# Four blocks over 32 images: the 32x128 TensorE tiling replaced by 64-row and strip forms, rounding moved from ScalarE to GpSimd

## The chip, the core and the metric

One NeuronCore of a Trainium2 chip runs the whole program; the other seven are idle. The metric is the device time of one execution in microseconds (us). TensorE (PE) does the matmuls, VectorE (DVE), ScalarE (ACT) and GpSimd (POOL) the elementwise work, and SyncE (SP) issues the DMAs.

## The reference

The input `x` is 32 images of 128 channels by 1024 positions (fp32). Each image goes through four blocks:

```
L0: xn = group_norm(x, 8 groups);  q,k,v = xn Wq, xn Wk, xn Wv (+bias), width 128
    x  = softmax(q k^T / sqrt(128)) v Wp + bp + xn
L1: t  = group_norm(x, 32 groups); 8 heads of width 16
    x  = concat_h softmax(q_h k_h^T / 4) v_h  Wp + bp + x
L2: h  = instance_norm(x);         one head of width 128
    x  = x + softmax(q k^T / sqrt(128)) v
L3: Qn, Kn = l2-normalised 16-wide projections over channels; V = 128-wide projection
    x  = gamma * (sum_n V + Qn^T (Kn V^T)) / (N + Qn^T (sum_n Kn + eps))
```

## The kernel before

Everything of an image lives in SBUF as 128 partitions (channels) by 1024 columns (positions); the images are software-pipelined. Each image is cut into some 500 small steps, named in `STEPS`: `f_*` are the full-width attentions L0 and L2 (argument `layer` 0 or 2), `p_*`, `m_*`, `s_*`, `o_*` the eight-head attention L1, `t_*` the last block L3. The table `TIME` gives each step a moment relative to its image's start, and image i stands `PERIOD` later than image i-1. `play()` sorts all steps of all images by that moment, and each engine issues its own part of each step in that order. So the table sets only the order in which each in-order engine meets its work; semaphores do the rest.

PSUM is shared by name: `P_CHAIN` (one bank) holds all small products in turn, `P_MAX` the scores of which only the row maximum is wanted, `P_SC` and `P_FULL` scores and outputs of the full-width attentions, `P_HEAD` and `P_ACC` those of the heads. A TensorE step waits until the step before it on the same bank has been read (`chain_free`, `max_free`), so a late reader holds up TensorE and all that is queued on it.

Precision. Two kinds of matmul occur. Where the operands are fp32r (rounded fp32) a matmul is one pass over its columns. Where they are plain fp32, the trace has two records for one matmul and the columns are streamed four times. The full-width attentions use split operands: `hi` is the value rounded to fp32r and `lo` the remainder, and a product is hi·hi + hi·lo + lo·hi. For each half of q, k and v (steps `f_qk`/`f_value`, and `p_qk` for the heads) TensorE writes the projection into `P_CHAIN`; ScalarE reads it twice, once into `hi` (L827, L847, L863) and once into the single SBUF tile `exact` (L837, L854, L869); GpSimd then subtracts, `lo = exact - hi` (L719, L726, L752). `exact` is one tile for all: the next copy into it waits for the subtraction before.

TensorE tilings. A matmul whose operands fill only part of the 128x128 array is placed in a part of it. In this kernel four classes occur: 128x128 (full), 64x128 (`m_max`, `s_scores`: two head pairs side by side in the row halves), 128x32 (`s_pv`, `f_sums`, `m_turn`, `t_matrix`, `t_turn`: results of up to 32 partitions, four side by side in `s_pv`) and 32x128 (`o_spread`, `f_spread`, `t_ksum`, `t_out`: contractions over 16, 2 or 17 rows). In the profile's rows the pair before the shape (`17*128`, `128*17`) is rows times columns of the operand held in the array, from which the class follows.

L3 in short: `t_project` makes q, k, v per token, `t_matrix` sums k v^T over eight groups of 128 tokens into a 17x129 matrix, `t_keep` copies it to `ma`, `t_ksum`/`t_scale` make the divisor, `t_turn` transposes the scaled queries (eight 128x17 pieces), `t_out` multiplies `ma` by them.

Of the kernel before, what the change touches and what calls it, by code (L numbers as in the profile page):

```python
# [6 lines left out]
F32R = mybir.dt.float32r  # L7
# [4 lines left out]
C = 128  # L12
N = 1024
# [15 lines left out]
FULL_ROW = {0: 64, 2: 96}  # L29

PERIOD = 206.000
# [23 lines left out]
    t_ksum=(), t_scale=(), t_turn=(range(2),), t_turned=(range(2),), t_out=(range(2),),  # L55
# [3 lines left out]
    load=[-444.568],  # L59
    g_stat=[-342.954],  # L60
    g_average=[-329.385],
    g_var=[-327.831],
    g_apply=[-327.403],
    f_qk=[-324.62, 236.025, -318.173, 237.463, -316.071, 239.499, -307.845, 240.328],
# [12 lines left out]
    f_scores=[-263.28, 268.702, -261.043, 270.662, -258.57, 285.892, -252.49, 288.403, -250.371,
        290.772, -247.938, 299.63, -242.481, 304.009, -237.548, 308.313, -228.304, 316.719,
        -222.89, 321.314, -216.238, 323.033, -213.85, 329.623, -209.464, 331.03, -206.509, 334.796,
        -204.968, 343.181, -191.73, 346.525],  # L80
    f_less=[-266.355, 269.509, -263.662, 270.173, -262.719, 281.768, -260.687, 289.64, -256.216,
        291.082, -245.343, 298.521, -241.05, 301.934, -238.661, 302.674, -229.65, 308.912,
        -228.073, 317.519, -222.928, 321.041, -219.107, 323.554, -214.199, 325.222, -204.373,
        329.575, -195.645, 335.975, -187.214, 341.895],
    f_exp=[-268.223, 264.621, -258.987, 269.397, -257.31, 277.163, -251.224, 287.023, -247.696,
        292.071, -247.182, 295.201, -244.469, 301.093, -241.845, 302.139, -235.507, 308.569,
        -231.815, 311.103, -229.246, 316.026, -215.475, 316.504, -209.673, 321.277, -201.534,
        325.812, -188.334, 331.546, -185.442, 335.653],
    f_plo=[-253.636, 261.779, -247.912, 262.733, -243.882, 285.896, -243.223, 290.654, -242.148,
        293.919, -240.27, 300.114, -238.771, 307.496, -237.402, 308.425, -236.979, 309.735,  # L90
        -232.01, 318.166, -230.727, 318.184, -230.13, 334.62, -224.858, 343.112, -204.25, 347.219,
        -187.48, 350.979, -178.415, 355.211],
    f_add=[-233.808, 279.161, -251.331, 262.822, -244.056, 290.409, -242.413, 291.769, -242.043,
        295.383, -240.22, 303.539, -237.966, 307.617, -237.194, 309.239, -279.97, 258.722,
        -234.087, 310.608, -231.148, 318.787, -229.752, 335.525, -205.881, 344.174, -195.077,
        347.242, -194.2, 355.122, -191.606, 358.969],
    f_pv=[-258.564, 276.685, -252.295, 276.718, -249.065, 291.543, -246.2, 295.985, -241.646,
        304.458, -235.005, 308.326, -228.594, 317.236, -222.453, 320.625, -214.672, 323.529,
        -213.821, 330.323, -209.242, 331.088, -205.083, 337.021, -201.343, 345.473, -187.722,
        349.286, -176.874, 350.007, -172.212, 352.561],  # L100
# [25 lines left out]
    m_max_read=[-85.592, -82.44, -80.627, -73.34, -72.457, -68.925, -63.823, -62.141, -60.424,  # L126
# [1416 lines left out]
```

## Time and profile before

| | us |
|---|---|
| three runs | 6186.26, 6187.2, 6193.69 (median 6187.2) |
| the profiled execution, its own time | 6179.77 |
| its span, first to last instruction | 6178.0 |
| mean granted TensorE clock | 0.979 |
| HBM read / written | 18.13 MB / 16.78 MB |

The profile is one execution. "Busy" counts the time in which an engine has an instruction in flight; TensorE's ends are modelled, so two neighbouring matmuls overlap in the rows and the distance from one start to the next is what one costs.

### The profile page before, as it was taken

What the parts mean: (1) busy time and instruction counts of PE and PEld (TensorE: products, weight loads), DVE (VectorE), ACT (ScalarE), POOL (GpSimd) and SP (SyncE); (2) the same over time, 40 slices, a digit from 0 to 9 for tenths busy, and PEclk for the clock granted to TensorE, in tenths of its full rate; (3) what the DMA queues carried; (4) which work ended last, traced back from release to release, by engine and by line L of the source; (5) the groups of instructions that cost most, each with busy time, mean ns of one, the idle gap of its engine ahead of it and who ended that gap; (6) DMA issues with size and microseconds to landing.
All of it is one profiled execution on the core that took longest, in us unless ns stands there. A gap on an engine that the chain in (4) does not pass through costs nothing.

```text
span 6178.0 us, 82441 instructions
## 1 busy us (share of the span) xinstructions
PE 5741.7 (93%) x28818; PEld 2690.0 (44%) x28818; DVE 4620.2 (75%) x5748; ACT 4141.6 (67%) x5764; POOL 3426.0 (55%) x2739
## 2 busy tenths in 40 slices
PE   5789999999999999999999999999999999999885
PEld 2334444444444444444444444444444444444332
DVE  2677777777777777777777777777777777777752
ACT  2367777766777676777766767767677777677652
POOL 4336655556665555655555666555565555566433
PEclk7899999999999999999999999999999999999996
DMA  1011101011101101111101110110110110111000
GB/s 36 4 27 24 29 21 30 20 31 24 31 19 30 31 20 31 24 25 25 29 21 31 24 31 19 30 30 21 31 24 21 29 30 20 31 24 31 16 17 8
DMA packets 103485, 154.27 MB, mean 25 GB/s; under 512 B 63776, under 2 KB 66080, under 8 KB 102944
## 3 DMA queue, kind: packets, MB, share of 16 engines
q1 hardware_dynamic: 103072, 149.00, 11.1%
q8 instruction: 230, 3.77, 0.3%
q14 instruction: 183, 1.50, 0.1%
HBM read 18.13 MB, written 16.78 MB: 6 GB/s over the span
## 4 chain that ended last, share of the span: by engine, by line
PE 72%; DVE 16%; ACT 5%; issue 3%; POOL 3%; DMA 0%; SPq 0%; DVEq 0%; POOLq 0%; ACTq 0%
PE p_max L1251 16%; PE p_chain L1251 15%; PE p_sc L1251 12%; PE p_full L1251 11%; PE p_acc L1251 9%; PE p_head L1251 8%; DVE mx_half L1066 8%; ACT p L930 3%; DVE f2mx L1061 2%; DVE fp L1107 2%; POOL x L787 1%; POOL fsum L781 1%; POOL fp_lo L760 1%; DVE f_num L1125 1%; DVE t_dn L1198 1%
## 5 line engine op out<-in xcount | busy, mean ns | idle before, releaser
L1066 DVE TENSOR_REDUCE mx_half<-p_max 128x2 f32<-128x1024 f32 x2048 | 2506.8, 1224 | 891.1 <-PE p_max L1251 883.1
L930 ACT ACTIVATE p<-p_head 128x1024 f32<-128x1024 f32 x2048 | 2094.8, 1023 | 1103.0 <-PE p_head L1251 1047.8
L760 POOL TENSOR_TENSOR fp_lo<-fp,fp_hi 128x512 fp32r<-128x512 f32 x1024 | 1311.6, 1282 | 734.1 <-ACT fp L894 732.5
L781 POOL TENSOR_TENSOR fsum<-fsum,fp 128x512 f32<-128x512 f32 x768 | 987.9, 1286 | 282.3 <-ACT fp L894 282.1
L1251 PE MATMUL p_max<-ks,qs 63*128 63x512 f32 x4096 | 993.9, 481 | 102.0 <-DVE mx_half L1066 80.3
L1251 PE MATMUL p_acc<-p,v 128*17 128x512 f32 x8192 | 1080.9, 601 | 7.8 <-ACT p L930 7.6
L1251 PE MATMUL p_head<-qs,ks 64*128 64x512 f32 x4096 | 938.9, 454 | 43.6 <-ACT p L930 26.5
L892 ACT ACTIVATE fp_hi<-fp 128x512 fp32r<-128x512 f32 x1024 | 641.4, 626 | 367.3 <-DVE fp L1107 261.6
L1107 DVE TENSOR_TENSOR fp<-p_sc,f_shifts 128x512 f32<-128x512 f32 x1024 | 700.1, 684 | 147.5 <-PE p_sc L1251 60.3
L1251 PEld LDWEIGHTS p_max<-ks,qs 63*128 63x128 f32 x4096 | 385.8, 185 | 921.5 <-DVE mx_half L1066 736.3
L1251 PEld LDWEIGHTS p_head<-qs,ks 64*128 64x128 f32 x4096 | 385.7, 185 | 679.5 <-issue 385.8
L894 ACT ACTIVATE fp<-fp 128x512 f32<-128x512 f32 x1024 | 634.2, 619 | 0.0
L1061 DVE TENSOR_REDUCE f0mx<-p_max 128x1 f32<-128x1024 f32 x256 | 312.2, 1220 | 136.4 <-PE p_max L1251 136.2
L777 POOL TENSOR_TENSOR fsum<-fp 128x512 f32<-128x512 f32 x128 | 164.1, 1282 | 427.6 <-ACT fp L894 427.6
L1061 DVE TENSOR_REDUCE f2mx<-p_max 128x1 f32<-128x1024 f32 x256 | 312.5, 1221 | 104.2 <-PE p_max L1251 104.2
L1251 PEld LDWEIGHTS p_acc<-p,v 128*17 128x17 f32 x8192 | 144.6, 95 | 328.3 <-issue 282.2
L1251 PE MATMUL p_sc<-f2q_hi,f2k_hi 128*128 128x512 f32 x512 | 253.6, 495 | 35.0 <-DVE fp L1107 31.3
L1251 PE MATMUL p_sc<-f0q_hi,f0k_hi 128*128 128x512 f32 x512 | 251.0, 490 | 19.9 <-DVE fp L1107 17.9
L1251 PE MATMUL p_full<-fp_hi,f0v_hi 128*128 128x512 f32 x512 | 242.6, 474 | 2.7 <-POOL fp_lo L760 2.7
L1251 PE MATMUL p_full<-fp_hi,f2v_hi 128*128 128x512 f32 x512 | 228.7, 447 | 5.9 <-POOL fp_lo L760 5.9
L1251 PE MATMUL p_max<-f2k_hi,f2q_hi 128*128 128x512 f32 x512 | 187.7, 448 | 29.2 <-DVE f2mx L1061 17.4
L1251 PE MATMUL p_max<-f0k_hi,f0q_hi 128*128 128x512 f32 x512 | 185.2, 444 | 24.8 <-DVE f0mx L1061 17.2
(187 smaller groups left out, 7977.6 us busy)
## 6 DMA issues: line engine op xcount, KB each, us to landing
qs<-cq_hi SPq DMA_DIRECT2D x128, 256.0 KB, 4.8
ks<-ck_hi SPq DMA_DIRECT2D x128, 256.0 KB, 4.7
x_in<-x_dram SPq DMA_DIRECT2D x32, 512.0 KB, 4.4
qs<-cq_lo SPq DMA_DIRECT2D x64, 256.0 KB, 4.4
ks<-ck_lo SPq DMA_DIRECT2D x64, 256.0 KB, 5.1
out_dram<-x SPq DMA_DIRECT2D x32, 512.0 KB, 5.3
o<-o SPq DMA_DIRECT2D x256, 32.0 KB, 2.0
zrow<-rz SPq DMA_DIRECT2D x128, 16.0 KB
```

Source lines behind the costliest of these rows:

```text
L760: pool.tensor_tensor(fp_lo[u % 2][:, :], fp[u % 2][:, :], f32(fp_hi[u % 2][:, :]), ALU.subtract).then_inc(f.plo, 1)
L777: pool.tensor_tensor(dst, fp[(u - 1) % 2][:, :], fp[u % 2][:, :], ALU.add)\
L781: pool.tensor_tensor(dst, dst, fp[u % 2][:, :], ALU.add).then_inc(f.sum, 1)
L787: pool.tensor_tensor(x3[:, :], f_num[:, :], x2[:, :], ALU.add)\
L892: act.activation(fp_hi[u % 2][:, :], fp[u % 2][:, :], ACT.Exp, scale=float(C) ** -0.5).then_inc(f.p, 1)
L894: act.activation(fp[u % 2][:, :], fp[u % 2][:, :], ACT.Exp, scale=float(C) ** -0.5).then_inc(f.pexact, 1)
L930: act.activation(p1[slot][:, 2 * pr:2 * pr + 2, :], P_HEAD[:, :].rearrange("p (e n) -> p e n", e=2), ACT.Exp, scale=float(DH) ** -0.5).the ...
L1061: dve.reduce_max(f_mx[layer][:, v:v + 1], P_MAX[:, :], AX.X).then_inc(sem.max_read, 1)
L1066: dve.reduce_max(mx_half[:, pr, :, t, kh], P_MAX[:, :].rearrange("p (e n) -> p e n", e=2), AX.X)\
L1107: dve.tensor_tensor(fp[u % 2][:, :], P_SC[:, :], f_shifts[:, :], ALU.add)\
L1125: dve.tensor_tensor(f_num[:, q], f_num[:, q], P_CHAIN[:, :], ALU.mult)\
L1251: return pe.matmul(dst, lhsT, rhs, start=start, stop=stop)
```

## The change

It does four things.

1. No matmul uses 32x128 any more. `f_spread` and `o_spread` contract over 64 rows (zero rows are added: `zrow` and `spread_r` become 128 rows, the two layers share rows 64 and 65). `t_matrix` writes its matrix four times, once into each 32-column strip; `t_keep` copies all 128 rows; the new GpSimd step `t_spots` multiplies the matrix by four masks (`strips`) into `ma_spots`; `t_turn` becomes two full 128x128 transposes of queries padded to 32; `t_out` becomes four full matmuls of 128 columns for each half.
2. `mm32` writes an fp32 matmul as four 32-column strips where the matmul before it in the order was of the class 128x32, and as one full matmul otherwise.
3. ScalarE makes only the `exact` copy of a projection; GpSimd first rounds `exact` into `hi` (a new instruction, CAST) and then subtracts for `lo`. This holds for all sixteen projection halves of an image.
4. All numbers of `TIME` are new (of the table one or two lines are shown), `PERIOD` is 205.92 for 206.0, and two semaphores per layer become one counter `sc_read`. `wq1`, `wk1`, `ma` and half of `neg` move into unused columns of `cw`.

```diff
-PERIOD = 206.000
+PERIOD = 205.920
-    f_lo=[-323.302, 231.815, -319.877, 242.954, -312.981, 243.248, -310.103, 253.328],
+    f_lo=[134.208, 690.504, 137.952, 694.248, 140.136, 698.928, 142.944, 704.232],
-    t_turn=[396.761, 400.053],
+    t_turn=[858.672],
...
-        spread_r = sb("spread_r", [SPREAD, C], F32R)
+        spread_r = sb("spread_r", [C, C], F32R)
+        strips = sb("strips", [C, G1])
...
             def f_lo(b, u, layer):
                 f, dst = full(layer), (f_q if u < 2 else f_k)[layer]
+                pool.wait_ge(sem.chain, chain_left("f_hi", b, u, layer))
+                if u == 0:
+                    after(pool, (f.sc, b.shift(-1), PER.f_sc, 2 * T))
+                pool.tensor_copy(dst[0][:, half(u % 2)], exact[:, :]).then_inc(f.hi, 1)
                 pool.wait_ge(f.hi, b.at(PER.f_hi, u + 1))
-                pool.wait_ge(sem.chain, chain_left("f_hi", b, u, layer))
                 pool.tensor_tensor(dst[1][:, half(u % 2)], exact[:, :],
                                    f32(dst[0][:, half(u % 2)]), ALU.subtract).then_inc(f.lo, 1)
...
+            def t_spots(b):
+                pool.wait_ge(sem.chain, chain_left("t_keep", b))
+                after(pool, (sem.t_o, b.shift(-1), PER.t_o, 2))
+                pool.tensor_tensor(ma_spots[:, :, :],
+                                   ma.rearrange("p (a c) -> p a c", a=1).broadcast_to([C, G1, C]),
+                                   strips[:, :].rearrange("p (j a) -> p j a", a=1)
+                                   .broadcast_to([C, G1, C]), ALU.mult).then_inc(sem.t_sp, 1)
...
             def f_hi(b, u, layer):
...
-                act.activation(dst[0][:, h], P_CHAIN[:, :], ACT.Identity, bias=col(bias))\
-                   .then_inc(f.hi, 1)
                 if u:
                     act.wait_ge(f.lo, b.at(PER.f_lo, u))
...
+            def mm32(dst, lhsT, rhs):
+                if tiling[0] != "columns":
+                    return mm(dst, lhsT, rhs)
+                for j in range(C // STRIP):
+                    strip = slice(STRIP * j, STRIP * (j + 1))
+                    last = mm(dst[strip, :], lhsT[:, strip], rhs, tiles="columns")
+                return last
...
-                mm(P_CHAIN[:, :], ones_r[r, :], zrow[r, half(h)]).then_inc(f.rb, 1)
+                mm(P_CHAIN[:, :], spread_r[r, :], zrow[r, half(h)], tiles="rows").then_inc(f.rb, 1)
...
                 for t in range(T):
-                    last = mm(P_CHAIN[0:D3 + 1, 0:C + 1], ka[:, t, :], tm[:, t, 2 * D3:W3 + 1],
-                              start=t == 0, stop=t == T - 1)
+                    for j in range(G1):
+                        last = mm(P_CHAIN[STRIP * j:STRIP * j + D3 + 1, 0:C + 1], ka[:, t, :],
+                                  tm[:, t, 2 * D3:W3 + 1], start=t == 0, stop=t == T - 1,
+                                  tiles="columns")
...
-            def t_turn(b, h):
+            def t_turn(b):
                 pe.wait_ge(sem.t_qs, b.at(PER.t_qs, 1))
-                chain_free("t_turned", b, h)
-                for t in range(T // 2):
-                    last = mm(P_CHAIN[0:D3 + 1, tile(t)], t_dn[:, 4 * h + t, :], mat("ident"))
+                chain_free("t_turned", b)
+                for h in range(2):
+                    last = mm32(P_CHAIN[:, tile(h)],
+                                t_dn[:, 4 * h:4 * h + 4, :].rearrange("p t d -> p (t d)"),
+                                mat("ident"))
...
-                mm(P_CHAIN[:, :], ma[:, 0:C], qt3[:, 4 * h:4 * h + 4, :]).then_inc(sem.t_o, 1)
+                for j in range(G1):
+                    last = mm32(P_CHAIN[:, tile(j)], ma_spots[:, j, :], qt3[:, h, :])
+                last.then_inc(sem.t_o, 1)
```

How the order changes, at three places. The rows are of the built programs: line of the kernel, operation, output and inputs by name, size of the output, and how often it stands there in a row. First TensorE in the last block L3, from `t_ksum` (`p_chain<-cw,ma`) to the first half of `t_turn` (`p_chain<-cw,t_dn`); before:

```order
L1251 MATMUL p_chain<-cw,ma 128x17
L1251 MATMUL p_head<-qs,ks 128x512 x2
L1251 MATMUL p_acc<-p_0,v_0 17x512 x4
L1251 MATMUL p_max<-ks,qs 128x512 x2
L1251 MATMUL p_head<-qs,ks 128x512 x2
L1251 MATMUL p_chain<-cw,t_dn 17x128 x4
```

and now:

```order
L1297 MATMUL p_chain<-cw,ma_sum 128x17
L1297 MATMUL p_head<-qs,ks 128x512 x2
L1297 MATMUL p_max<-ks,qs 128x512 x2
L1297 MATMUL p_sc<-f0q_hi,f0k_hi 128x512
L1297 MATMUL p_sc<-f0q_lo,f0k_hi 128x512
L1297 MATMUL p_sc<-f0q_hi,f0k_lo 128x512
L1297 MATMUL p_full<-fp_hi,f0v_hi 128x512
L1297 MATMUL p_full<-fp_lo,f0v_hi 128x512
L1297 MATMUL p_full<-fp_hi,f0v_lo 128x512
L1297 MATMUL p_head<-qs,ks 128x512 x2
```

Behind these ten rows the new order has eleven more of the same kinds (score and output matmuls of the heads and of L0) before the transpose `p_chain<-cw,t_dn 128x128 x2`; where four rows stood between the two chain steps, twenty stand now.

Second, TensorE at the projections of L2, from the second half of q (`p_chain<-hx,cw`, the second of four) on; before:

```order
L1251 MATMUL p_chain<-hx,cw 128x512
L1251 MATMUL p_head<-qs,ks 128x512 x2
L1251 MATMUL p_max<-ks,qs 128x512 x2
L1251 MATMUL p_chain<-hx,cw 128x512
L1251 MATMUL p_full<-fp_hi,f0v_hi 128x512
L1251 MATMUL p_full<-fp_lo,f0v_hi 128x512
L1251 MATMUL p_full<-fp_hi,f0v_lo 128x512
```

and now:

```order
L1297 MATMUL p_chain<-hx,cw 32x512 x4
L1297 MATMUL p_max<-ks,qs 128x512 x2
L1297 MATMUL p_full<-fp_hi,f0v_hi 128x512
L1297 MATMUL p_full<-fp_lo,f0v_hi 128x512
L1297 MATMUL p_full<-fp_hi,f0v_lo 128x512
L1297 MATMUL p_head<-qs,ks 128x512 x2
L1297 MATMUL p_max<-ks,qs 128x512 x2
L1297 MATMUL p_chain<-hx,cw 128x512
L1297 MATMUL p_head<-qs,ks 128x512 x2
L1297 MATMUL p_max<-ks,qs 128x512 x2
L1297 MATMUL p_chain<-hx,cw 128x512
```

The second projection is written as strips, since a `p_acc` row stands just ahead of it; the three output matmuls now stand ahead of the third projection, and the fourth follows the third with two pairs of score matmuls between them.

Third, GpSimd at the same projections; before:

```order
L719 TENSOR_TENSOR f2q_lo<-exact,f2q_hi 128x512
L760 TENSOR_TENSOR fp_lo<-fp,fp_hi 128x512
L719 TENSOR_TENSOR f2q_lo<-exact,f2q_hi 128x512
L719 TENSOR_TENSOR f2k_lo<-exact,f2k_hi 128x512 x2
L752 TENSOR_TENSOR f2v_lo<-exact,f2v_hi 128x512
```

and now:

```order
L752 CAST f2q_hi<-exact 128x512
L754 TENSOR_TENSOR f2q_lo<-exact,f2q_hi 128x512
L752 CAST f2q_hi<-exact 128x512
L754 TENSOR_TENSOR f2q_lo<-exact,f2q_hi 128x512
L752 CAST f2k_hi<-exact 128x512
L754 TENSOR_TENSOR f2k_lo<-exact,f2k_hi 128x512
L752 CAST f2k_hi<-exact 128x512
L754 TENSOR_TENSOR f2k_lo<-exact,f2k_hi 128x512
L794 CAST f2v_hi<-exact 128x512
L797 TENSOR_TENSOR f2v_lo<-exact,f2v_hi 128x512
```

The `fp_lo` row that stood between the first two subtractions has moved ahead of the group, and each subtraction has a CAST ahead of it.

## Rows read from the trace of the kernel before

**Rows 1.** The page, part 1: busy time, share of the span, instructions.

```profile
PE 5741.7 (93%) x28818; PEld 2690.0 (44%) x28818; DVE 4620.2 (75%) x5748; ACT 4141.6 (67%) x5764; POOL 3426.0 (55%) x2739
```

**Rows 2.** Timeline, PE: start us, length us, line, operation, [idle before].

```profile
1938.12 0.28 PE L1251 MATMUL p_chain<-g_mv,cw 128*128 128x2 f32 x2
...
4131.87 0.28 PE L1251 MATMUL p_chain<-g_mv,cw 128*128 128x2 f32 x2
```

**Rows 3.** Windows: length, busy us of each engine (instructions), PEclk, DMA share, GB/s.

```profile
1938.10:2120.80 182.70, 175.91 (x901) 83.02 (x900) 144.35 (x180) 129.15 (x181) 106.72 (x86) 1.00 0.12 26
```

**Rows 4.** Waits of PE, 1938.1 to 2120.8: total us, times, longest.

```profile
PE p_chain L1251 <- DVE t_dn L1209: 0.7, 1, 0.7
PE p_chain L1251 <- ACT exact L837: 0.6, 1, 0.6
```

**Rows 5.** Timeline of PE, 2020 to 2059: starts at changes of tiling.

```profile
2022.32 1.91 PE L1251 MATMUL p_acc<-p,v 128*17 128x512 f32 x16
2024.16 0.51 PE L1251 MATMUL p_max<-ks,qs 63*128 63x512 f32 x2
...
2048.33 1.05 PE L1251 MATMUL p_acc<-p,v 128*17 128x512 f32 x8
2049.32 1.12 PE L1251 MATMUL p_chain<-tm,ma 17*128 17x512 f32 x2
2050.37 0.50 PE L1251 MATMUL p_max<-ks,qs 63*128 63x512 f32 x2
2050.80 0.50 PE L1251 MATMUL p_sc<-f0q_hi,f0k_hi 128*128 128x512 f32 x1
...
2054.42 0.50 PE L1251 MATMUL p_full<-fp_hi,f0v_hi 128*128 128x512 f32 x1
...
2056.01 0.50 PE L1251 MATMUL p_head<-qs,ks 64*128 64x512 f32 x2
...
2056.68 0.50 PE L1251 MATMUL p_full<-fp_hi,f0v_hi 128*128 128x512 f32 x1
...
2057.57 0.49 PE L1251 MATMUL p_chain<-zrow,spread_r 16*128 16x512 f32 x1
2058.00 0.50 PE L1251 MATMUL p_head<-qs,ks 64*128 64x512 f32 x2
```

**Rows 6.** Timeline of PE: small fp32 matmuls.

```profile
2041.41 1.05 PE L1251 MATMUL p_chain<-cw,t_dn 128*17 128x128 f32 x8
2042.39 0.49 PE L1251 MATMUL p_head<-qs,ks 64*128 64x512 f32 x2
...
2067.98 0.61 PE L1251 MATMUL p_chain<-fsum,ones 128*1 128x256 f32 x8
...
2118.49 1.16 PE L1251 MATMUL p_chain<-cw,hx 128*128 128x128 f32 x8
2119.58 0.49 PE L1251 MATMUL p_max<-ks,qs 63*128 63x512 f32 x2
```

**Rows 7.** Timeline of all engines, 2071.5 to 2075: one projection of L2.

```profile
2071.83 1.02 PE L1251 MATMUL p_chain<-hx,cw 128*128 128x512 f32 x2
...
2072.89 0.69 ACT L827 ACTIVATE f2q_hi<-p_chain,cw 128x512 fp32r<-128x512 f32 x1 [0.34 <-PE p_chain L1251]
...
2073.47 0.68 ACT L837 ACTIVATE exact<-p_chain,cw 128x512 f32<-128x512 f32 x1
...
2074.29 1.27 POOL L719 TENSOR_TENSOR f2q_lo<-exact,f2q_hi 128x512 fp32r<-128x512 f32 x1 [4.60 <-ACT exact L837]
```

**Rows 8.** Groups by line, whole span: count, busy us, mean ns, idle before.

```profile
L760 POOL TENSOR_TENSOR fp_lo<-fp,fp_hi 128x512 fp32r<-128x512 f32 x1024 | 1311.6, 1282 | 734.1 <-ACT fp L894 732.5
L781 POOL TENSOR_TENSOR fsum<-fsum,fp 128x512 f32<-128x512 f32 x768 | 987.9, 1286 | 282.3 <-ACT fp L894 282.1
...
L690 POOL MEMSET o<- 128x512 f32 x1 | 0.5, 524 | 0.0
...
L1066 DVE TENSOR_REDUCE mx_half<-p_max 128x2 f32<-128x1024 f32 x2048 | 2506.8, 1224 | 891.1 <-PE p_max L1251 883.1
```

More of the change, by code:

```diff
@@ L54 @@
     t_project=(range(3),), t_tokens=(range(3),), t_norms=(), t_keys=(), t_matrix=(), t_keep=(),
-    t_ksum=(), t_scale=(), t_turn=(range(2),), t_turned=(range(2),), t_out=(range(2),),
+    t_spots=(), t_ksum=(), t_scale=(), t_turn=(), t_turned=(), t_out=(range(2),),
     t_leave=(range(2),), store=())
 TIME = dict(
[L59 to L64, printed above, removed]
@@ new lines @@
+    f_move=[229.368, 749.472, 286.776, 802.512],
+    f_sums=[266.496, 810.624],
+    f_row=[273.048, 804.384],
+    f_gather=[201.288, 720.456],
+    f_recip=[276.792, 808.128],
+    f_return=[202.848, 721.08],
+    f_spread=[289.272, 818.112, 294.576, 823.416],
+    f_divide=[288.024, 813.12, 290.208, 816.864],
+    p_stat=[291.768],
+    p_average=[299.256],
+    p_var=[298.944],
+    p_apply=[302.376],
+    p_qk=[312.048, 313.92, 315.48, 320.472],
+    p_hi=[303.312, 304.56, 306.744, 309.552],
@@ new lines @@
+    o_return=[491.136, 591.288],
+    o_move=[516.72, 576.936],
+    o_spread=[667.104, 669.912],
+    o_divide=[673.968, 678.648],
+    o_project=[672.096, 674.904],
+    o_residual=[680.52, 683.328],
+    i_stat=[685.2],
+    i_apply=[686.448],
+    f_out=[824.976],
+    t_project=[828.72, 831.528, 837.768],
+    t_tokens=[828.096, 832.152, 833.4],
+    t_norms=[835.272],
+    t_keys=[845.568],
+    t_matrix=[848.688],
+    t_keep=[842.448],
+    t_spots=[863.352],
+    t_ksum=[851.808],
+    t_scale=[849.624],
@@ L181 @@
+    t_turn=[858.672],
+    t_turned=[857.112],
+    t_out=[860.232, 869.592],
+    t_leave=[861.792, 864.6],
+    store=[849.936])
 CHAIN_READER = dict(g_average="g_var", p_average="p_var", f_qk="f_hi", p_qk="p_hi",
@@ L325, in __init__ @@
         self.base = new(f"f{layer}_base")
-        self.based = new(f"f{layer}_based")
-        self.less = new(f"f{layer}_less")
         self.sc = new(f"f{layer}_sc")
@@ L405, in __init__ @@
         self.t_tr = new("t_tr")
+        self.t_sp = new("t_sp")
         self.t_o = new("t_o")
@@ L689, in _ @@
             pool.memset(zpad[:, :, :], 0.0).then_inc(s_ones, 1)
+            pool.memset(t_dn[:, :, :], 0.0).then_inc(s_ones, 1)
+            pool.memset(f32(spread_r[:, :]), 0.0).then_inc(s_ones, 1)
             pool.memset(o1[0][:, 0:HALF], 0.0).then_inc(s_ones, 1)
@@ L723, in p_lo @@
                 dst = cq if u < 2 else ck
+                pool.wait_ge(sem.chain, chain_left("p_hi", b, u))
+                if u == 0:
+                    for g in range(2):
+                        after(pool, (sem.stacked[g], b.shift(-1), PER.stacked, PER.stacked))
+                pool.tensor_copy(dst[0][:, half(u % 2)], exact[:, :]).then_inc(sem.p_hi, 1)
                 pool.wait_ge(sem.p_hi, b.at(PER.p_hi, u + 1))
-                pool.wait_ge(sem.chain, chain_left("p_hi", b, u))
                 pool.tensor_tensor(dst[1][:, half(u % 2)], exact[:, :],
@@ L1249, in _, with mm @@
         def _(pe):
-            def mm(dst, lhsT, rhs, start=True, stop=True):
+            tiling = ["full"]
+            def mm(dst, lhsT, rhs, start=True, stop=True, tiles="full"):
+                tiling[0] = tiles
                 return pe.matmul(dst, lhsT, rhs, start=start, stop=stop)
+            def mm32(dst, lhsT, rhs):
[5 more added lines that the diff above has]
+                return last
             def chain_free(reader, b, *args):
@@ L1320, in m_max @@
                     r = head_rows(e, SHIFT_ROW)
-                    last = mm(P_MAX[:, half(e)], qs[r, pr, tile(t)], ks[r, pr, half(kh)])
+                    last = mm(P_MAX[:, half(e)], qs[r, pr, tile(t)], ks[r, pr, half(kh)],
+                              tiles="rows")
                 last.then_inc(sem.m_s, 1)
@@ L1340, in s_scores @@
                     last = mm(P_HEAD[:, half(e)], ks[rows, pr, tile(kt)],
[L1341 removed]
+                              qs[rows, pr, half(r % 2)], tiles="rows")
                 last.then_inc(sem.s_sc, 1)
@@ L1419, in f_sums @@
                     part = slice(j * N // 4, (j + 1) * N // 4)
-                    last = mm(P_CHAIN[32 * j:32 * j + 1, 0:N // 4], ones[:, 0:1], fsum[:, part])
+                    last = mm(P_CHAIN[32 * j:32 * j + 1, 0:N // 4], ones[:, :], fsum[:, part],
+                              tiles="columns")
                 last.then_inc(f.z, 1)
             def f_spread(b, h, layer):
-                f, r = full(layer), slice(FULL_ROW[layer], FULL_ROW[layer] + 2)
+                f, r = full(layer), slice(HEAD_ROWS, 2 * HEAD_ROWS)
                 if h == 0:
```

334 lines of the change are left out of this document (166 added, 168 removed), and 48 rows, old and new, of tables (m_max, m_max_read, s_exp, s_scores).

## The prediction

> **What bounds the kernel now.** I read the page first: TensorE is busy 93% of the span, VectorE 75%, ScalarE 67%, GpSimd 55% [rows 1]. Busy TensorE is only a hint, since its ends are modelled, so I look for the period. The small matmul `g_average` comes once an image; between its rows at 1938.12 and 4131.87 lie twelve images [rows 2], so one image costs 182.8 us, and 32 of them 5850 of the 6178; the other 328 are filling and draining. The window of one image has TensorE busy for 175.9 of 182.7 us at a granted clock of 1.00 (its 2.4 GHz level), VectorE 144, ScalarE 129, GpSimd 107 [rows 3]. The waits of TensorE in that window over 0.15 us add up to some 5.5 us, two of which matter below: 0.7 us for `t_dn` and 0.6 us for the `exact` copy [rows 4]. So TensorE's own work sets the period, and what counts is how long its in-order queue takes.
>
> **What a change of tiling costs.** The timeline shows it as a fixed part of each stretch of one class. Full: six fp32r passes take 2054.42 to 2056.01 = 1.59 us, three take 2056.68 to 2057.57 = 0.89, so three cost 0.70 and a stretch 0.19. 64x128: two pairs take 2056.01 to 2056.68 = 0.67, one takes 2050.37 to 2050.80 = 0.43, so 0.24 a pair and 0.19 a stretch. 128x32: two groups take 1.84 from 2022.32, one takes 0.99 from 2048.33, so 0.85 a group and 0.14 a stretch. 32x128: a lone pass takes 2057.57 to 2058.00 = 0.43, less 0.23 for a pass, 0.20 a stretch; `t_out` 2049.32 to 2050.37 = 1.05, so 0.85 for its four passes [rows 5].
>
> **The change, part by part, for one image.**
>
> Stretches. Counted in the built order of a middle image, there were 78 of 64x128, 56 full, 36 of 128x32 and 9 of 32x128; now 77, 57, 33 and none. That saves 9 x 0.20 + 3 x 0.14 + 0.19 - 0.19 = 2.2 us. The `f_spread` and `o_spread` passes themselves go beside 64-row work at about the same 0.23, at no gain.
>
> `t_turn`: each half took 0.98 (2041.41 to 2042.39), 0.84 without the fixed part, two halves 1.68. Now it is two full fp32 matmuls of 128 columns. Four such take 2118.49 to 2119.58 = 1.09 less 0.19 = 0.90 [rows 6], so two cost 0.45: 1.2 us saved. `t_out`: twice 0.85 becomes eight matmuls at 0.225 = 1.8: 0.1 lost. `t_matrix`: 8 matmuls become 32, four side by side as `p_acc`'s are; if they pack as those do, no cost (see the rivals). Strips by `mm32`: a group of four costs 0.85, a full one 0.85 too; they stand in about two places an image. TensorE work in all: 3.35 us less.
>
> Waits that go. The wait of 0.7 for `t_dn` had 2.3 us of other work to cover it, by these prices; the new order has 7.8 there. The wait of 0.6 at the third L2 projection is replaced by what follows.
>
> ScalarE drops sixteen reads of a bank at 0.6 to 0.7 each, some 10 us; costed at nothing, as it idles 53 us of an image anyway. POOL takes on sixteen CASTs and `t_spots`, at most 16 x 1.28 + 1.3 = 22 us, and stays near 70% busy; that too is hidden as long as it is only throughput.
>
> The wait that comes. The loop through `exact` gets longer. In the trace the matmul starts at 2071.83, ScalarE's first read at 2072.89 (1.06 later), the `exact` copy at 2073.47, the subtraction at 2074.29 (0.82 later) for 1.28 [rows 7, 8]. The next copy had to wait 2.1 us after the one before. Now it is 0.82 + CAST + 1.28 + about 0.1 for two handovers = 2.2 + CAST. No CAST of this size is in the trace. Below: a GpSimd memset of 128x512 takes 0.52. Above: a two-input operation takes 1.28, and it takes that whether it writes fp32r (1282 ns) or fp32 (1286 ns), so rounding by itself is free [rows 8]. A CAST has one input; I take 0.6, near the memset, and keep 0.5 to 1.28 for the range. The Trainium skill (GPSIMD Engine Reference, 3.1) gives a simple body 1.03 cycles an element at 1.2 GHz, 0.44 us here; by that, an estimate, the forecast would be 0.8 us an image lower, 6086; no row shows it.
>
> With 0.6 a loop takes 2.8 us. In the new order the six L2 projections (four of q and k, two of v) stand, by the prices above, at 0, 2.5, 5.5, 7.2, 10.3 and 12.3 us, and the next user of the bank, `f_spread`, at 13.8. The copies can start at 1.06 + 2.8k: the sixth at 15.1, done at 15.7. TensorE waits 15.7 - 13.8 = 1.9 us. The L1 projections stand at 0, 3.1, 4.8, 8.6 and 10.8 with two other GpSimd operations between them: the fourth copy ends at 10.7, no wait. Those of L0 stand at 0, 2.4, 6.2, 10.6, 14.0, 16.7, next 19.6: no wait. Behind ScalarE's later copies stand the exponentials of the heads; I put 0.15 for what they are late.
>
> **Sum.** -3.35 - 0.7 - 0.6 + 1.9 + 0.15 = -2.6 us an image, 83 us for 32. In filling and draining nothing covers the CASTs: six or seven on the way in and as many on the way out, +8. Against the profiled execution's span of 6178.0 that is 6103; its own time is 1.8 above its span, 6105, and the median of the runs lies 7.4 above that execution, so **6112**.
>
> **Rivals.** A measurement of this kernel can tell about 0.2%, 12 us, from no change.
>
> *A, the forecast*, 6070 to 6165: 0.60.
>
> *B, the new wait is absorbed.* If VectorE and ScalarE use those 1.9 us to get ahead, waits later in the image shrink by as much. -4.65 an image, + 8: 6046. For it: ScalarE's relief. Against it: the waits that remain are short and spread out. 0.12.
>
> *C, slower: the CAST is dear.* At 1.28 the loop is 3.5 us: the sixth L2 copy ends at 19.2, a wait of 5.4; L1 waits 1.8 at `p_value`, and L0, with `fp_lo` and `fsum` between its subtractions, about 1: 8.2 instead of 1.9. Less 1 us absorbed elsewhere, +2.5 an image, and 16 for filling and draining: 6285. It decides from a CAST of 0.88 us on (6.3 us of wait for 0.68 us of CAST). Against it: the memset, and the one input. 0.11.
>
> *D, the order takes it back.* All of `TIME` is new. The loop TensorE, `P_MAX`, VectorE has 80 turns an image, each with 1.22 us of reduction [rows 8] and the matmuls before it, and that engine has 38 us to spare. Counting where less work than one loop stands between two `P_MAX` steps, both orders come to the same 5.7 us an image; this speaks against D. Should other waits grow by 2.6, there is no change: 6187. 0.09.
>
> *E, `t_matrix` is bound by issue.* It now needs 64 records in the 1.7 us that 16 took, 27 ns each. The densest in the trace is `f_sums`, eight in 0.61 less 0.14, 59 ns each [rows 6], though its columns alone explain that. At 59 ns it takes 3.8 us, +2.1 an image: 6179, within the bound of no change. The Trainium skill (TensorE: Matmul & The Clock Gate, Part 1) gives 62 ns for a matmul that the sequencer decodes in software, which would make the same; no run here tells whether this program's are. 0.08.
>
> **How the numbers follow.** 6112 is A. The range 6045 to 6190 holds A, nearly all of B, D and E, and leaves out C and the tails. Faster: A and B and the lower part of D and E, 0.77; within 0.2%: 0.11; slower: C and a little of D, 0.12.
>
> **What would show it.** The distance between `g_average` rows should be 180.2 us. Rows with `16*128`, `2*128` or `17*128` should be gone, `t_turn` should take 0.45 to 0.65 us, `t_matrix` 1.7 to 1.9. CAST should read near 600 ns; over 880 C is right. The waits should show TensorE held by the `exact` copies (lines 886 and 907 of the changed kernel) for about 2 us an image, and none for `t_dn`. A period at or above 182.8 with a CAST near 600 would mean that D or E holds, and if 32x128 stretches are gone and the period falls by under 1.5 us with no new wait, the fixed part of a stretch isn't what I take it for.

## The result and the profile after

The changed kernel takes **6200.41 us** (median of 19 runs, 6192.24 to 6219.49), the kernel before 6187.2 (19 runs): ratio 1.0024, 95% interval 1.0018 to 1.003. It is slower by 0.24%: a small difference, but the interval leaves equality out. The forecast was 6112, with a range of 6045 to 6190.

The profiled execution took 6192.78 us, its span is 6191.0, its mean clock 0.96 (0.979 before). First the page's busy times, against [rows 1]:

```profile
PE 5734.2 (93%) x30756; PEld 2763.2 (45%) x30756; DVE 4679.1 (76%) x5750; ACT 3844.4 (62%) x5252; POOL 3775.8 (61%) x3286
```

ScalarE lost its sixteen reads, GpSimd has the CASTs, as described. From image 5 to the last the mean distance of `g_average` rows is 183.55 us; before it was 182.80. Windows of the changed kernel, against [rows 3]: one image, then three pieces inside it (columns: length, busy us of PE, PEld, DVE, ACT, POOL with instructions, PEclk, DMA share, GB/s):

```profile
2126.22:2308.89 182.67, 175.08 (x962) 84.99 (x961) 145.88 (x180) 119.86 (x165) 117.69 (x102) 0.98 0.12 26
2238.34:2241.55 3.21, 0.97 (x5) 0.48 (x4) 3.14 (x5) 0.02 (x1) 2.50 (x2) 0.88 0.09 20
2241.55:2247.62 6.07, 6.07 (x16) 3.35 (x16) 3.31 (x5) 2.15 (x3) 2.50 (x2) 0.50 0.05 9
2247.62:2256.34 8.72, 8.59 (x52) 3.15 (x50) 8.13 (x10) 6.29 (x9) 3.62 (x3) 1.00 0.00 1
```

The third row is what the prediction did not have: for 6 us of this image TensorE runs at a granted clock of 0.50, its 1.2 GHz level. The clock records show it once in each of the 27 steady images, for 6.8 or 10.2 us, 215 us in all; the kernel before has none in its own 27. TensorE's waits in the image, against [rows 4] (total us, times, longest):

```profile
PE p_sc L1297 <- DVE fp L1145: 2.2, 1, 2.2
PE p_max L1297 <- DVE mx_half L1104: 1.9, 6, 0.4
PE p_chain L1297 <- ACT exact L907: 0.6, 1, 0.6
```

The first is a single wait of 2.2 us (1.7 to 2.4 over the 27 images), and the slow stretch belongs to it. In this image the clock fell some 0.8 us before the wait ended (0.88 over the 3.21 us of the second window); over the 27 images it fell 0.9 to 4.3 us after TensorE had stopped. The timeline there, PE:

```profile
2237.90 0.51 PE L1297 MATMUL p_max<-ks,qs 63*128 63x512 f32 x2 [0.21 <-DMA ks<-ck_lo]
2238.34 0.50 PE L1297 MATMUL p_full<-fp_hi,f0v_hi 128*128 128x512 f32 x1
...
2241.55 0.80 PE L1297 MATMUL p_sc<-f0q_hi,f0k_hi 128*128 128x512 f32 x1 [2.24 <-DVE fp L1145]
...
2247.62 0.40 PE L1297 MATMUL p_chain<-zrow,spread_r 64*128 64x512 f32 x1
```

And what VectorE did meanwhile, with GpSimd and SyncE:

```profile
2235.82 0.36 DVE L1113 TENSOR_TENSOR mx<-mx_half 128x32 f32<-128x32 f32 x1
2238.15 0.35 DVE L1176 RECIPROCAL rz<-zt 128x32 f32<-128x32 f32 x1 [1.96 <-DMA zt<-o]
2238.54 1.13 DVE L1179 CAST rz<-rz 128x32 fp32r<-128x32 f32 x1
2239.70 1.20 DVE L1181 TENSOR_TENSOR rz<-rz 128x32 fp32r<-128x32 f32 x1
2240.82 0.68 DVE L1145 TENSOR_TENSOR fp<-p_sc,f_shifts 128x512 f32<-128x512 f32 x1
...
2238.35 1.28 POOL L805 TENSOR_TENSOR fp_lo<-fp,fp_hi 128x512 fp32r<-128x512 f32 x1 [2.21 <-ACT fp L932]
2239.59 1.26 POOL L826 TENSOR_TENSOR fsum<-fsum,fp 128x512 f32<-128x512 f32 x1
...
2234.30 1.08 SPq L657 DMA_DIRECT2D zt<-o  x1
```

VectorE came to `o_recip` (three small instructions on `zt`) 2 us before its DMA had landed. Then its two small operations from SBUF to SBUF, a CAST and a TENSOR_TENSOR of 32 columns (0.18 and 0.20 us in the kernel before at this step; called the two copies below), took 1.13 and 1.20, each ending with a GpSimd instruction. So VectorE lost 1.96 us to the DMA and 1.95 to the copies. Behind them in the queue stood the `f_less` that frees `P_SC` for TensorE. In the kernel before, this second `o_recip` of an image waited for nothing (in 26 of the 27 images; 0.16 us in the other).

The terms of the forecast can be read beside this: `t_turn`, `t_matrix` and the new wait for `exact`.

```profile
2226.06 0.71 PE L1297 MATMUL p_chain<-cw,t_dn 128*128 128x128 f32 x4
2226.53 0.48 PE L1297 MATMUL p_full<-fp_hi,f0v_hi 128*128 128x512 f32 x1
...
2215.19 1.96 PE L1297 MATMUL p_chain<-tm,ka 128*17 128x129 f32 x64
2216.97 1.04 PE L1297 MATMUL p_acc<-p,v 128*17 128x512 f32 x8
...
2260.19 1.02 PE L1297 MATMUL p_chain<-hx,cw 128*128 128x512 f32 x2
...
2276.21 0.47 PE L1297 MATMUL p_chain<-zrow,spread_r 64*128 64x512 f32 x1 [0.59 <-ACT exact L907]
```

### The profile page after: what moved, and what is told of

Read it like the earlier page. It is cut to its first block, busy times and chain, and to the rows that moved or that the text cites. A ratio compares the mean times of both kernels' runs of the same rounds, so it can differ in the third digit from the quotient of the medians.

```text
span 6191.0 us, 86420 instructions
## 1 busy us (share of the span) xinstructions
PE 5734.2 (93%) x30756; PEld 2763.2 (45%) x30756; DVE 4679.1 (76%) x5750; ACT 3844.4 (62%) x5252; POOL 3775.8 (61%) x3286
## 4 chain that ended last, share of the span: by engine, by line
PE 73%; DVE 14%; DMA 4%; issue 3%; ACT 3%; POOL 1%; SPq 1%; DVEq 0%; POOLq 0%; ACTq 0%
PE p_max L1297 16%; PE p_chain L1297 14%; PE p_full L1297 12%; PE p_sc L1297 12%; PE p_head L1297 10%; PE p_acc L1297 10%; DVE mx_half L1104 7%; ACT p L968 2%; DVE f2mx L1099 2%; DMA zt<-o 2%; DVE f_num L1163 1%; DVE fp L1145 1%; DVE x L1170 1%; DVE rz L1179 1%; DMA zrow<-rz 1%
## 5 line engine op out<-in xcount | busy, mean ns | idle before, releaser
L1297 PE MATMUL p_head<-qs,ks 64*128 64x512 f32 x4096 | 1014.3, 472 | 49.7 <-ACT p L968 39.1
L1297 PEld LDWEIGHTS p_head<-qs,ks 64*128 64x128 f32 x4096 | 407.2, 189 | 693.2 <-ACT p L968 407.8
L886 ACT ACTIVATE exact<-p_chain,cw 128x512 f32<-128x512 f32 x256 | 176.2, 688 | 218.2 <-PE p_chain L1297 100.1
L1297 PE MATMUL p_chain<-hx,cw 128*128 128x512 f32 (+1 forms) x698 | 286.8, 628 | 14.0 <-ACT hx L864 5.4
L1297 PE MATMUL p_full<-fp_hi,f0v_hi 128*128 128x512 f32 x512 | 255.6, 499 | 5.3 <-POOL fp_lo L805 5.3
```

The lines of the kernel that those rows point to most:

```text
L886: act.activation(exact[:, :], P_CHAIN[:, :], ACT.Identity, bias=col(bias))\
L1297: return pe.matmul(dst, lhsT, rhs, start=start, stop=stop)
```

## The experiments

Theory S: one place holds the loss. `o_recip` comes too early in VectorE's new order, TensorE stops for 2.24 us, and the clock falls behind that stop. Rivals: D, the new order is worse all over; T, the clock falls because of the small fp32 matmuls ahead; and for the long copies P (held by GpSimd) against Q. Times are medians; ratios are to the kernel before on the same chip, with 95% intervals; a period is the mean distance of the `g_average` rows from image 5 to image 32 of the profiled execution, 27 steady images.

**a_recip_late** and **a_chain_late**: `o_recip` behind the `f_less`, without and with the steps that depend on it.

```diff
+TIME["o_recip"][1] += 11.0
```
```diff
+TIME["o_recip"][1] += 11.0
+TIME["o_spread"][0] += 2.9
+TIME["o_spread"][1] += 2.7
...
+TIME["f_qk"][1] += 2.0
```

> The changed kernel; only VectorE's second o_recip stands later, behind the f_less, the m_neg and the reduction that stood behind it. Theory S (one stall): in the trace of the changed kernel o_recip waits 1.96 us for its DMA, then 1.13 + 1.20 us in two 32-column copies, and TensorE waits 2.24 us for the f_less behind it; 1 to 2 us after that wait begins the granted clock is 0.50 for 6.8 to 10.2 us, once an image. With f_less in front that wait goes, but the same numbers now reach the o_spread matmul some 2 us later against an unmoved place, so TensorE should wait 2 to 3.5 us there (for the zrow DMA), the clock should still fall, a few us later, and the period should stay within 182.5 to 185 us, 6160 to 6240. Theory D (the whole order is a little worse, this place has no special part): the wait is removed like any other, -1 to -2 us an image, about 6150. Theory T (the clock falls because of the small fp32 matmuls t_turn and t_out just ahead of it, not because of a wait): the clock falls at the same place in the order, ahead of or at the same f_scores, although TensorE doesn't wait there; period 181.4 (2.24 less).

> As a_recip_late, and the steps that depend on o_recip stand some 2.5 us later on TensorE and VectorE too (o_spread, o_divide, o_project, o_residual, the L2 projections 1 to 2 us). Theory S: no wait of TensorE over 1.5 us is left there, the clock stays at 1.00 through the whole image, the period falls by 2.24 and by the 2.5 to 3.5 us that the slow clock costs, to 178 to 179.5 us, the time to 6020 to 6070, below both kernels. Theory D: other waits take its place, 182 to 183, 6160 to 6190. Theory T: the clock still falls once an image behind t_out; 181 to 182, 6110 to 6150.

Measured: 6246.74 us (1.0095, 1.0079 to 1.0111), period 184.43; and 6520.88 (1.0536, 1.052 to 1.0552), period 193.58. TensorE's wait for the `f_less` is gone in both, and a longer one stands behind it; timeline of PE of the first, then of PE and SyncE of the second:

```profile
2263.75 0.64 PE L1299 MATMUL p_chain<-zrow,spread_r 64*128 64x512 f32 x1 [4.61 <-DMA zrow<-rz]
```
```profile
2344.63 0.79 PE L1313 MATMUL p_head<-qs,ks 64*128 64x512 f32 x2 [4.97 <-DMA qs<-cw]
...
2341.32 1.28 SPq L691 DMA_DIRECT2D zrow<-rz  x2
2342.65 0.56 SPq L668 DMA_DIRECT2D qs<-cw  x1
```

The first wait is 1.1 us longer than I had allowed, and the time 7 us over the range. The clock falls in each of the 27 images of the first again, but now behind the new wait: it follows the wait, not the place in the order, which speaks against T. Delaying `o_recip` was no cure. On SyncE's queue the DMAs of `o_return` stand ahead of `m_row` (in the kernel before, behind it), so a late `o_recip` also held back the row that the next head scores need. I had predicted 6020 to 6070 for the second; that queue is what I had left out. The clock falls 53 times in its 27 images, and TensorE also waits longer for `p` and for the reductions; how its 10 us more an image divide among these I have not traced.

**b_recip_one** and **b_recip_two**: the kernel before, with its `o_recip` two and three steps earlier.

```diff
+TIME["o_recip"][1] += -4.8
```
```diff
+TIME["o_recip"][1] += -5.8
```

> The kernel before; only VectorE's second o_recip stands two steps earlier, ahead of m_both and the f_less. It must then wait about 1 us for its DMA, and the f_less about 1.4 us longer. Theory S: TensorE waits 1.5 to 1.8 us for that f_less once an image where it waited 0.27. If a wait of that length is enough for the clock to fall, +1.3 and some 3 us an image, 6320; if it isn't, +1 us, 6215. Theory D: VectorE makes up for it, 6187 to 6200. Theory T: the clock doesn't fall.

> The kernel before; VectorE's second o_recip stands one reduction earlier still, as long a wait as in the changed kernel or longer. Theory S: TensorE waits 2.5 to 3.3 us once an image, the granted clock falls to 0.50 for some 7 us behind it in every image as in the changed kernel, +5 to +6 us an image, 6350 to 6380. Theory D: +1 to +2 us an image, 6220 to 6250. Theory T: the waits cost their own length at most and the clock stays at 1.00, 6270.

Measured: 6247.69 us (1.0099, 1.0082 to 1.0116) and 6323.1 (1.0219, 1.0201 to 1.0236), periods 184.71 and 187.10. PE's timeline of the first:

```profile
2254.90 0.41 PE L1253 MATMUL p_chain<-cw,mx 128*32 128x128 f32 x2 [1.52 <-DVE mx L1077]
```

and of the second, with windows over the wait and behind it:

```profile
2284.56 0.41 PE L1253 MATMUL p_chain<-cw,mx 128*32 128x128 f32 x2 [2.82 <-DVE mx L1077]
```
```profile
2281.74:2284.56 2.82, 0.00 (x2) 0.00 (x1) 2.11 (x6) 0.00 (x0) 0.00 (x0) 1.00 0.17 38
2286.30:2289.70 3.40, 3.40 (x10) 1.93 (x10) 1.79 (x2) 1.21 (x3) 2.51 (x2) 0.50 0.08 14
```

The wait alone, put into the kernel before by one number, brings the slow stretch with it: behind 2.82 us in 22 of 27 images, behind 1.52 us in 6. Nothing else of the change is in this kernel, and with the clock falling theory T is out. The sizes were off: the first time lies between the two that I had given for S (6215 and 6320), the second 27 us under its range. The stretch was shorter than in the changed kernel (3.4 us in 15 of the 22), hence 4.3 us an image and not 5 to 6. The same trace has the price of the clock without that of the wait: the 22 images with a slow stretch last 187.4 us, the 5 without one 185.6.

**a_pv_early** and **a_pv_early_act**: the numbers reach `o_recip` earlier. ScalarE idled 2.2 us ahead of the last exponential of an image, which stood behind an `f_exp`.

```diff
+TIME["s_exp"][63] += -2.0
+TIME["s_pv"][30] += -6.1
+TIME["s_pv"][31] += -6.0
+TIME["s_out"][3] += -1.0
```

The second one has this too:

```diff
             def o_gather(b, g):
+                if g == 1:
+                    return
...
             def s_out(b, r):
...
+                if r == 3:
+                    act.wait_ge(sem.o_ev, b.at(PER.o_ev, 4))
+                    act.dma_start(zt[:, 1, :], o1[1][DH::32, :]).then_inc(sem.o_z, 16)
```

> The changed kernel; the last exponential of an image stands ahead of the f_exp before it (ScalarE idles 2.21 us there in the changed kernel), the last two s_pv 2 us earlier on TensorE, the last s_out ahead of the next f_exp. The table alone. o_gather's DMA stands on SyncE's queue behind the DMAs of stack, of which the last was issued at 2232.89 + 1.22, so it can come no more than 0.2 us earlier than now. Theory S (one stall at the f_less behind o_recip, made by the time at which the DMA zt lands): the stall stays near 2 us and the clock falls; period 183 to 184, 6175 to 6215. Theory O (the place is set by s_out's time, the queue plays no part): stall under 1 us, no slow clock, 178.5 to 180, 6030 to 6080.

> As a_pv_early, and the DMA that gathers zt is issued by ScalarE right behind its s_out, not by SyncE behind the DMAs of stack. zt should land 1.5 to 2 us earlier than in the changed kernel, when VectorE comes to o_recip, and GpSimd has nothing to do at that time, so the two 32-column copies should take 0.2 us each, not 1.13 and 1.20. Theory S: TensorE's wait for that f_less is under 0.7 us, the granted clock stays at 1.00 through a steady image, the period falls by some 5 us to 178 to 179.5 us, the time to 6020 to 6070, below both kernels. Theory D (the order as a whole is worse, other waits take its place): 181.5 to 183, 6130 to 6190. Theory T (the clock falls because of what stands ahead, not because of a wait): the wait is gone but the clock still falls once an image; 180.5 to 182, 6090 to 6150.

Measured, one run each: 6084.24 and 6077.88 us, beside 6191.7 for the kernel before; periods 179.73 and 179.31. (**best**, below, contains the same edits and was run five times.) The timeline of DVE of a_pv_early_act, then of PE:

```profile
2205.74 0.34 DVE L1186 RECIPROCAL rz<-zt 128x32 f32<-128x32 f32 x1
2206.12 0.18 DVE L1189 CAST rz<-rz 128x32 fp32r<-128x32 f32 x1
2206.33 0.19 DVE L1191 TENSOR_TENSOR rz<-rz 128x32 fp32r<-128x32 f32 x1
...
2203.11 0.50 PE L1307 MATMUL p_max<-ks,qs 63*128 63x512 f32 x2 [1.49 <-DVE mx_half L1114]
```

No wait for the DMA, short copies, no wait at the `f_less`. Four numbers of the table give back 3.8 us an image. The table alone nearly does it, so SyncE's queue was not the hindrance that I had expected in the first (theory O there was right). What remains is a new wait of 1.49 us between two `m_max`, behind which the clock falls in 12 of 27 images of the first and 9 of the second. I had expected no slow clock, and the times lie 4 us over the range of theory O and 8 us over that of S. In a_pv_early_act the images with a fall last 180.3 us, those without 178.8, with the same wait in both: 1.5 us is the price of the 3.4 us at the low clock.

**a_add_late**: one `f_add` of GpSimd a step later in the changed kernel, so that GpSimd is idle during the second copy.

```diff
+TIME["f_add"][24] += 1.2
```

> The changed kernel; only one of GpSimd's f_add (the one that ran from 2239.59 to 2240.85 while VectorE's second small copy of rz took 1.20 us) stands one step later, behind the next f_plo. Theory P (VectorE's small operations from SBUF to SBUF are held as long as a GpSimd instruction runs): with GpSimd idle there the second takes 0.19 us, the first still 1.13, the f_less comes 1.0 us earlier, TensorE's wait is 1.2 to 1.4 us instead of 2.24, and the granted clock falls in few of the images, as behind the 1.5 us waits of b_recip_one and a_pv_early: period 180 to 181.5 us, the time 6080 to 6130. Theory Q (they are long for another reason, the DMA's writes or the engine's own): the second still takes about 1.2 us, wait and clock as in the changed kernel, 183 to 184, 6190 to 6210.

Measured: 6157.79 us (0.9952, 0.9937 to 0.9968), period 181.83. DVE and POOL:

```profile
2225.62 0.35 DVE L1178 RECIPROCAL rz<-zt 128x32 f32<-128x32 f32 x1 [2.24 <-DMA zt<-o]
2226.01 0.87 DVE L1181 CAST rz<-rz 128x32 fp32r<-128x32 f32 x1
2226.91 0.19 DVE L1183 TENSOR_TENSOR rz<-rz 128x32 fp32r<-128x32 f32 x1
...
2225.55 1.28 POOL L807 TENSOR_TENSOR fp_lo<-fp,fp_hi 128x512 fp32r<-128x512 f32 x1 [2.23 <-ACT fp L934]
```

Theory P holds: the second copy takes 0.19 instead of 1.20, the first still ends with the GpSimd instruction beside it (2226.88 and 2226.83). TensorE's wait for the `f_less` falls to 1.00 in this image, with one of 0.52 two matmuls ahead of it; over the 27 images it is 1.2 on the mean, where the changed kernel has 2.15. So about half of that wait came from the two copies' delay. The time misses my 6080 to 6130: the clock still falls in 21 of 27 images, not in few.

**best**: a_pv_early_act with the two `m_max` set apart. On it, three parts of the change are undone one at a time.

```diff
+TIME["m_max"][30] += -2.9
+TIME["f_less"][22] += 1.7
```

> a_pv_early_act with m_max 30 ahead of the f_scores it followed (and its reduction ahead of the f_less), so that no two m_max stand one behind the other; there TensorE waited 1.49 us for the reduction and the granted clock was 0.50 for 3.4 us in about one image of three. Theory S: no wait over 0.9 us left in a steady image, the clock stays at 1.00, period 177.8 to 178.7 us against 179.13, the time 6035 to 6065. Theory D (a wait removed comes back elsewhere): period 179 to 179.5, 6070 to 6085.

Measured: 6075.52 us (6068.2 to 6078.81), ratio **0.9808** (0.9795 to 0.9822), the lowest time of all, level with a_pv_early_act and below both kernels. Period 179.61 with 3 falls of the clock in 27 images. Against a_pv_early_act nothing is gained beyond the spread: theory D, that a wait removed here comes back elsewhere, holds, and the time lies 11 us over the range given for S. The wait of 1.49 us is gone, but a GpSimd instruction runs again beside the first copy (0.94 us in place of 0.18), and TensorE waits 0.5 us an image for the row that comes of it (`zrow`), which it doesn't in a_pv_early_act. Its windows, one image, and the stretch of the order (an `f_scores` to the second `o_spread`) that took 6.07 us at the low clock:

```profile
2094.18:2273.66 179.48, 172.94 (x962) 83.53 (x961) 145.20 (x180) 119.94 (x165) 117.55 (x102) 1.00 0.12 27
...
2208.22:2212.37 4.15, 3.61 (x17) 1.90 (x15) 2.84 (x4) 2.18 (x3) 4.15 (x4) 1.00 0.07 14
```

4.15 us with a wait of 0.51 in it, 3.64 of work: in the changed kernel, at 0.50, the same matmuls took 2.43 us more.

**best_full**, **best_rows32**, **best_scalar**:

```diff
-                if tiling[0] != "columns":
+                if True:
```
```diff
-                mm(P_CHAIN[:, :], spread_r[0:HEAD_ROWS, :], zrow[0:HEAD_ROWS, half(h)], tiles="rows")\
+                mm(P_CHAIN[:, :], spread_r[0:SPREAD, :], zrow[0:SPREAD, half(h)], tiles="rows")\
...
-                f, r = full(layer), slice(HEAD_ROWS, 2 * HEAD_ROWS)
+                f, r = full(layer), slice(HEAD_ROWS, HEAD_ROWS + 2)
```
```diff
-                pool.tensor_copy(dst[0][:, half(u % 2)], exact[:, :]).then_inc(f.hi, 1)
...
+                act.activation(dst[0][:, h], P_CHAIN[:, :], ACT.Identity, bias=col(bias))\
+                   .then_inc(f.hi, 1)
```

> best without strips: mm32 always makes one full 128x128 matmul. By the forecast's fixed part of 0.14 to 0.19 us for a stretch and about two strips an image between 128x32 work, each place gains a full stretch and a 128x32 one: +0.3 to +0.7 us an image, +10 to +22 us. If a stretch costs nothing: the same time as best within 5 us.

> best with the six spreads of an image (four f_spread, two o_spread) as 32x128 passes again, of 2 and 16 rows, not as 64-row ones beside 64x128 work. By the forecast's fixed part each is a stretch of its own again, 6 x 0.20 us, and may cut a 64x128 stretch in two, 6 x 0.19: +1.2 to +2.3 us an image, +38 to +75 us. If the fixed part belongs to something else than the change of row tiling: within 10 us of best.

> best with the rounding of the projections back on ScalarE (two reads of the bank each, the low part on GpSimd as before). If the longer loop through exact, 2.8 us with its CAST of 0.61 on GpSimd, costs what the waits for exact in the profile of the changed kernel say, 0.6 to 0.8 us an image, the period falls by that, -20 to -26 us. If ScalarE's relief of some 10 us an image paid, the waits for its p and exact grow by 0.5 to 2 us an image instead, +15 to +65 us. The forecast had a wait of 1.9 us an image for the longer loop (-60 us without it).

| | median us | ratio to before | period | against best |
|---|---|---|---|---|
| best_full | 6085.82 | 0.9829 (0.9816 to 0.9843) | 179.83 | +10 |
| best_rows32 | 6107.94 | 0.9864 (0.9851 to 0.9878) | 180.01 | +32 |
| best_scalar | 6117.72 | 0.9883 (0.9869 to 0.9896) | 180.59 | +42 |

The strips are worth about 10 us, at the low end of what was expected; the intervals of the ratios overlap, though every run of best_full (6084.01 and up) lies above every run of best (6078.81 and down). For the spreads the window of an image shows the work that was expected, against the 172.94 of best:

```profile
2106.72:2287.46 180.74, 174.28 (x962) 83.83 (x961) 146.23 (x180) 120.12 (x165) 117.51 (x102) 1.00 0.12 27
```

1.34 us more for six spreads, 0.22 each (1.2 at least was expected), but only 0.4 of it is left in the period, and the time is 6 us under the range. Part of the gap is the clock: best's three slow stretches, none of which best_rows32 has, add about 0.3 us to its period (its other 24 images last 179.3). And of the 26 us between the two profiled executions only 11 arise in the 27 steady images. best_scalar is slower, in the branch that I had for "ScalarE's relief pays" (+15 to +65) and not in the one on which the forecast stood. Its waits for `exact`, by line (total us, times, longest):

```profile
PE p_chain L1311 <- ACT exact L886: 31.9, 42, 1.4
PE p_chain L1311 <- ACT exact L903: 24.2, 36, 1.4
PE p_chain L1311 <- ACT exact L918: 23.6, 34, 0.7
```

79.7 us, 28.9 in best; in the steady images 1.9 us an image against 0.6. With two reads by ScalarE, one behind the other, the bank stays taken longer, and in this order that costs more than the CAST in the loop. The reservation matters: the order was made for one read. The kernel before, with two reads in an order of its own, waits only 0.6 us an image for `exact`, so what the move of the rounding is worth with the order fitted to either form is not shown.

## Why the prediction was wrong

**What bounds the kernel.** Right: the period decides, and TensorE's queue sets it.

**TensorE's work, -3.35.** Nearly right in sum: 175.91 us busy before [rows 3], 172.94 in best, -3.0. `t_turn` takes 0.47 (2226.06 to 2226.53; 0.45 forecast), `t_matrix` 1.78 (1.7 to 1.9; rival E is out). The fixed part of a 32x128 stretch, 0.20, comes back as 0.22 in best_rows32.

**Waits that go.** Right for `t_dn`, -0.7: no row for it is left in the image. The -0.6 for `exact` belongs to the next term.

**The new wait for `exact`, +1.9.** Mis-sized: 0.59. The loop was right. The CAST took 0.61 us (0.6 forecast), the sixth copy started 15.28 us behind the first projection (15.1 forecast). By the Trainium skill's 1.03 cycles an element (GPSIMD Engine Reference, 3.1) it would have been 0.44, an estimate for the elements alone; the trace doesn't agree. What failed is TensorE's side: `f_spread` would have been reached at 15.4, not at 13.8. Two waits for VectorE's reductions (0.34 and 0.33) stood in between; the other 0.9 of the difference I have not traced. The forecast's two terms (+1.9 for the wait that comes, -0.6 for the one that goes) had the move of the rounding as a loss of 1.3 us an image. In the steady images TensorE's waits for `exact` are 0.59 us an image before and 0.58 in the changed kernel: no loss at all.

**The step that failed: rival D, at 0.09.** The sum put what the new order costs at nothing. I had weighed the order by one loop only, the 80 turns of `P_MAX`, found both orders equal and took this as evidence against D. The order lost its time in another place. `o_recip` had been put where its DMA had not landed, on VectorE's in-order queue ahead of an `f_less` that TensorE needs. Taking the queue of each engine past each DMA-fed step could have found it: the order stands in the built program, and that `o_recip` came 3.1 us behind the issue of its DMA stood in the trace of the kernel before (it is 1.9 in the new order, without the wait). D as I had it (other waits grow by 2.6) was also mis-sized, since it had no term for the clock: [rows 3] show 1.00, and I took that as given. Nor had it a term for VectorE's small operations beside GpSimd's; GpSimd's work was costed as hidden, and the two copies held VectorE 1.95 us longer. The wait of 2.24 and 2.43 for the slow stretch make 4.7 us an image. The changed kernel loses 4.2 to a_pv_early_act (183.55 against 179.31): TensorE is busy 2.9 us longer, the slow stretch mostly, and idle 1.35 longer, since against the wait for the `f_less` (2.15 on the mean) stand waits for VectorE's reductions that are 1.4 shorter.

**Without that place** the gain on TensorE's work stands. By the means over the 27 steady images it is busy 3.2 us an image less from the kernel before to a_pv_early_act, slow stretches included. The sum fits too: -3.35 - 1.3 + 0.6 + 0.15 makes 178.9 from 182.8, and a_pv_early_act measures 179.3. But the fit is partly luck, because TensorE's idle time fell by 0.3 us only, from 6.8 to 6.55, and not term by term. The 0.7 for `t_dn` and 1.1 us of waits for VectorE's `f_less`, which the forecast didn't count, are gone; the waits for its reductions grew from 1.55 to 3.5. That last is rival D in a small form. Against 6112 the order with that place mended is 34 us faster, about what the idle time explains: it was forecast to grow by 0.75 us an image and fell by 0.3. The +8 for filling and draining can't be told: what is left of the span beside 32 periods is 328 us before and in best, 317 in the changed kernel and 338 in a_pv_early_act.

## What to carry to other kernels

Where an order of steps is renewed as a whole, go through each in-order queue for the steps that a DMA feeds and ask what stands behind them and who waits for that; one bad place can cost more than the change gives. In a kernel that keeps TensorE as busy as this one (93%), price a stop of TensorE at more than its length, and look at the granted clock in windows of one period, not only in the mean. Cure a late input where it is made, ahead of the step, before delaying the step and all that hangs on it.

## What the runs showed of the hardware that I had not expected

A stop of TensorE in otherwise dense work can bring the 1.2 GHz level. With one long wait an image, the clock fell in the 27 steady images this often: 27 times behind 2.24 us and 27 behind 4.61 us, 22 behind 2.82, 21 behind 0.52 and about 1.2 close together, 12 (a_pv_early) and 9 (a_pv_early_act) behind 1.49, 6 behind 1.52; never in the kernel before, whose longest wait in an image is 0.7. In best it fell in 3 images whose longest single waits were 0.6, 0.7 and 1.05. The length of a wait alone doesn't order them, since the same 1.49 us brings a fall in some images and not in others; what does is left open. A fall that lasted 3.4 us cost 1.5 us an image in a_pv_early_act; the longer one of the changed kernel cost 2.43 over the stretch shown.

Small VectorE operations from SBUF to SBUF can take as long as a GpSimd instruction. In the changed kernel 60 of the 64 CASTs of `rz` are more than 0.12 us over the shortest, 0.18 us, and each of the 60 ends within 0.15 us of the end of a GpSimd instruction; a_add_late showed for the TENSOR_TENSOR that this is the cause: 1.20 with a GpSimd instruction beside it, 0.19 in all 64 without. The reciprocal just ahead of them, 0.35 us, and the reductions of `P_MAX`, 1.22, were not lengthened. The Trainium skill has this rule (SBUF — State Buffer, "Who interferes with whom"): VectorE and GpSimd share a pair of ports, held for a whole instruction, by copies in a fast mode and by operations with two inputs in SBUF. The trace agrees for both kinds, in that both were held as long as the GpSimd instruction; which mode the CAST ran in no row shows. The prediction didn't use the rule, although the trace of the kernel before had its effect: 29 of its 64 CASTs of `rz` are long in the same way, at the first `o_recip` of an image. What the change did was to bring the second one beside GpSimd as well. The two instructions next to it are `fp_lo` and `fsum`, which the kernel before has too, so it was their new moment, and not a CAST of the projections, that held VectorE.
